# Graph network on one core: item widths chosen for two engines, and one-hots of eight small items made by one comparison

## What is computed

```python
def _graph_conv(x, src, dst, out_norm, in_norm, W, b):
    h = x * out_norm[:, None]
    agg = jax.ops.segment_sum(h[src], dst, num_segments=N_NODES)
    return agg * in_norm[:, None] @ W + b
# L0: three such layers with elu, the norms from the degrees of src and dst
# L1: msg = relu(x[src] + edge_attr @ W_edge.T + b_edge)
#     agg = segment_sum(msg, dst), then a two-layer MLP with batch norm
x = _layernorm(x + L0(x, ..., src, dst))
x = _layernorm(x + L1(x, [src, dst], edge_attr_16, ...))
```

## Time and profile before

| | |
|---|---|
| median of three runs | 6440.28 us |
| the profiled execution, own time | 6450.82 us |
| its span | 6449.1 us |
| preparation, up to the first evacuation | 123.2 us |
| counting stage | 123.2 to 2198.9 us |
| dense and gather stages | 2198.9 to 6449.1 us |
| PE busy in the span | 5397.2 us (84%) |
| DVE busy | 4675.9 us (73%) |
| POOL busy | 3568.3 us (55%) |
| ACT busy | 2313.7 us (36%) |

### The profile page before, as it was taken

One profiled execution on the slowest core, in us unless ns is written; L12 is line 12 of the kernel. 1 busy time (PEld: TensorE's weight loads), 2 busy tenths in 40 slices (PEclk: granted clock), 3 DMA queues, 4 the chain that ended last, 5 costly groups with the idle time before them and its releaser, 6 DMA issues.

```text
span 6449.1 us, 114582 instructions
## 1 busy us (share of the span) xinstructions
PE 5397.2 (84%) x38849; PEld 3248.0 (50%) x38893; DVE 4675.9 (73%) x18312; ACT 2313.7 (36%) x4022; POOL 3568.3 (55%) x3789
## 2 busy tenths in 40 slices
PE   5899997889987799999999999477787777777773
PEld 4456665556654455555555544244444444444442
DVE  4777789999999855565656622488888877777774
ACT  1776776787542100000000111243344433333331
POOL 7411112223220077777777777777777777777770
PEclk9999999999999999999999999799999988889885
DMA  2522223333211378888898987111111111111110
GB/s 81 228 96 98 83 87 114 137 119 135 86 63 52 109 264 286 279 267 278 273 274 271 281 299 260 35 44 44 43 44 43 44 41 41 41 41 41 41 39 20
DMA packets 434117, 825.45 MB, mean 128 GB/s; under 512 B 159529, under 2 KB 262981, under 8 KB 426709
## 3 DMA queue, kind: packets, MB, share of 16 engines
q1 hardware_dynamic: 305508, 713.91, 32.5%
q0 software_dynamic: 113632, 78.58, 5.5%
q10 hardware_dynamic: 14400, 25.61, 1.4%
HBM read 618.43 MB, written 199.35 MB: 127 GB/s over the span
## 4 chain that ended last, share of the span: by engine, by line
PE 37%; POOL 32%; DVE 15%; issue 11%; ACT 4%; DMA 1%; POOLq 0%; ACTq 0%; DVEq 0%
POOL rows_f L1058 26%; PE banks L2103 19%; DVE rows_f L1313 10%; PE banks L2025 7%; POOL sorted_recs L1023 5%; PE banks L1987 5%; DVE rows_f L1310 3%; ACT wide L1790 3%; PE banks L1994 2%; PE banks L2078 1%; PE banks L2085 1%; PE banks L2051 1%; PE banks L2335 1%; POOL tmp L934 1%; POOL hid L936 1%
## 5 line engine op out<-in xcount | busy, mean ns | idle before, releaser
L1058 POOL DMA_INDIRECT rows_f<-table,src_key x1725 | 1661.3, 963 | 525.5 <-issue 525.5
L1023 POOL DMA_INDIRECT sorted_recs<-onehot,rows x1280 | 1238.8, 968 | 533.4 <-issue 394.1
L1790 ACT ACTIVATE wide<-banks 128x784 fp8e4<-128x784 f32 x1563 | 1256.6, 825 | 737.3 <-PE banks L2025 733.8
L1313 DVE TENSOR_SCALAR rows_f<-rows_f,tmp 128x392 f16<-128x392 f16 (+2 forms) x5625 | 1409.5, 320 | 127.6 <-PE banks L2025 119.9
L2025 PE MATMUL banks<-rows_f 128*128 128x392 f16 (+1 forms) x6656 | 1237.6, 307 | 132.9 <-DVE rows_f L1313 124.5
L978 POOL DMA_INDIRECT onehot<-edge_runs_dram,rows_f x352 | 389.2, 1106 | 1447.5 <-DVE onehot L1166 1304.0
L2103 PE MATMUL banks<-wide,rows_f 128*128 128x512 fp8e4 (+1 forms) x4900 | 1127.4, 375 | 17.4 <-issue 12.2
L2025 PEld LDWEIGHTS banks<-rows_f 128*128 128x128 f16 x6656 | 858.6, 146 | 440.0 <-issue 163.1
L1987 PE MATMUL banks<-wide,onehot 128*128 128x392 fp8e4 x3125 | 792.6, 334 | 106.9 <-ACT wide L1790 98.7
L2192 PE MATMUL banks<-w_edge_blk,rows 80*128 80x320 f32 x690 | 293.6, 510 | 605.2 <-DVE rows_f L1610 523.9
L2103 PEld LDWEIGHTS banks<-wide,rows_f 128*128 128x128 f16 x4900 | 434.0, 98 | 396.0 <-issue 39.6
(11 more groups left out here) (334 smaller groups left out, 7046.6 us busy)
## 6 DMA issues: line engine op xcount, KB each, us to landing
wide<-counts SPq DMA_DIRECT2D x504, 896.0 KB
counts<-wide SPq DMA_DIRECT2D x50, 3136.0 KB, 9.8
rows_f<-table,src_key POOLq DMA_INDIRECT x1725
sorted_recs<-onehot,rows POOLq DMA_INDIRECT x1280
sorted_recs<-rows SPq DMA_DIRECT2D x28, 640.0 KB
rows<-attr_dram SPq DMA_DIRECT2D x345, 40.0 KB
onehot<-edge_recs_dram SPq DMA_DIRECT2D x143, 90.0 KB
agg_a<-attr_dram ACTq DMA_DIRECT2D x50, 250.0 KB
```

The costliest lines, as they stand in the source:

```text
L1023: G.indirect_dma_start(out=sorted_recs[:, :], out_offset=bass.IndirectOffsetOnAxis(ap=keys_of(t, t + 1).bitcast(I32), axis=0), in_=taken[g ...
L1058: G.indirect_dma_start(out=g_rows[:, n % ROW_RING, k, :], out_offset=None, in_=table32[:, :], in_offset=bass.IndirectOffsetOnAxis(ap=src_k ...
L1313: last = V.tensor_scalar(key, iota_key[:, 0:item.width * BLOCKS], key_cols[:, n:n + 1], None, ALU.is_equal)
L1790: A.activation(win_counts[o.half % 2][:, :, d0:d0 + o.quads * QUAD].rearrange("p b (q c) -> p b q c", c=QUAD), counted, ACT.Copy, scale=UN ...
```

## The change

Items have width 4, 2 or 1; width 8 is gone. `plan_half` takes, for each half, the least of the larger of two sums, one for each engine: items times the first number of `ITEM_COST`, and items times the second plus 4 for each node. Halves 48 to 40 keep width 4 and their items. Halves 39 to 10 have width 2 with 128 items each, 9 to 3 width 1 with 256 each, halves 2 and 1 width 2 with 256 and 337, and half 0 width 1 with 735. There are 7525 items in 59 chunks.

Items are made in **lots** of one width, 8 items (4 of width 4), in 3 buffers that hold lo and key. In a lot of width 2 or 1 one `tensor_tensor` makes all keys, with the items alternating in memory as the lo one-hots do; width 4 keeps `tensor_scalar` with contiguous columns. PE waits for a whole lot. The marks that DVE and ACT wait for are the ends of lots and octets.

Around it, more chunks ask for room: the rows are split between buffers, sets have 15 chunks, `near` is used twice, and SP loads `src_key` and `dst_key` after the search. With more items in the sparse halves, the places given by item number come at other halves: `edge_bounds` at half 30 (it was 23), `EXTREMES_TURN` 18 (21), `ROWS_TURN` 20 (27), `feature_tops` at half 26 (19), scans every 9 octets from octet 626 (every 7 from 849).

```diff
-UNITS_PER_BATCH = 6
-RING = 20
...
-ITEM_COST = {8: 14, 4: 10, 2: 9, 1: 8}
+ITEM_COST = {4: (31, 16), 2: (19, 8), 1: (14, 6)}
+NODE_COST = 4
...
-        cost = len(items) * ITEM_COST[width]
+        cost = max(len(items) * vector, len(items) * tensor + (hi - lo) * NODE_COST)
...
+LOT_CELLS, LOTS, LOT_BUFFERS = 4 * QCOLS, 8, 3
+
+SINGLE = 4
+
+
+def plan_lots():
+    lots, n = [], 0
+    while n < len(ITEMS):
+        width = ITEMS[n].width
+        size = min(LOTS, LOT_CELLS // (width * BLOCKS))
+        end = next((k for k in range(n, min(n + size, len(ITEMS))) if ITEMS[k].width != width), min(n + size, len(ITEMS)))
+        lots.append(Lot(n, end, width))
+        n = end
+    return lots
...
+MARKS = sorted({lot.end - 1 for lot in LOT_LIST} | {o.end - 1 for o in OCTETS})
...
-SETS = [(0, 1), (1, 2)] + [(c, min(c + 12, CHUNKS)) for c in range(2, CHUNKS, 12)]
+SETS = [(0, 1), (1, 2)] + [(c, min(c + 15, CHUNKS)) for c in range(2, CHUNKS, 15)]
...
+            if item.width == SINGLE:
+                key = key_ring[:, s, at * cells:(at + 1) * cells]
+            else:
+                key = lot_keys(s, cells)[:, :, at]
+            return item, lo_ring[:, s, :, at], key
+
+        def lot_keys(s, cells):
+            return key_ring[:, s, 0:cells * LOTS].rearrange("p (j n) -> p j n", n=LOTS)
...
-            rank(2 * P, SLOTS)
+            rank(2 * P, D0_SPLIT)
+            rank(D0_SPLIT, SLOTS)
...
-                if n % LOTS == 0:
-                    if lot_need(n):
-                        dve.wait_ge(s_used, lot_need(n))
-                    V.tensor_tensor(lo_ring[:, n // LOTS % LOT_BUFFERS, :, :], iota_lots,
-                                    lo_cols[:, n:n + LOTS].rearrange("p (o n) -> p o n", o=1).to_broadcast([P, P, LOTS]), ALU.is_equal)
                 item, lo, key = slot(n)
-                last = V.tensor_scalar(key, iota_key[:, 0:item.width * BLOCKS], key_cols[:, n:n + 1], None, ALU.is_equal)
-                if n in BATCH_TO:
-                    last.then_inc(s_pair, 1)
+                if n in LOT_FROM:
...
+                    if LOT_FROM[n] >= LOT_BUFFERS:
+                        dve.wait_ge(s_used, MARK_AT[LOT_LIST[LOT_FROM[n] - LOT_BUFFERS].end - 1])
+                    V.tensor_tensor(lo_ring[:, s, :, 0:size], iota_lots[:, :, 0:size],
+                                    lo_cols[:, n:lot.end].rearrange("p (o n) -> p o n", o=1).to_broadcast([P, P, size]), ALU.is_equal)
+                    if item.width != SINGLE:
+                        cells = item.width * BLOCKS
+                        V.tensor_tensor(lot_keys(s, cells)[:, :, 0:size], iota_keys[:, 0:cells, 0:size],
+                                        key_cols[:, n:lot.end].rearrange("p (o n) -> p o n", o=1).to_broadcast([P, cells, size]),
+                                        ALU.is_equal).then_inc(s_pair, 1)
+                if item.width == SINGLE:
+                    last = V.tensor_scalar(key, iota_key, single_cols[:, n:n + 1], None, ALU.is_equal)
+                    if n == lot.end - 1:
+                        last.then_inc(s_pair, 1)
...
-                    for q in range(item.at // QUAD, item.at // QUAD + units_of(item)):
...
+                    q, at = item.at // QUAD, item.at % QUAD * BLOCKS
+                    last = M(octet_ps[n % 2][:, q, at:at + item.width * BLOCKS], lo, key, start=fresh[q], stop=True, skip_group_check=True)
+                    fresh[q] = False
+                    if i in MARK_AT:
                         last.then_inc(s_used, 1)
```

More of the change, by code:

```diff
@@ L102, in plan_octets @@
     return [Octet(*o) for o in octets]
-def units_of(item):
-    return -(-item.width // QUAD)
 OCTETS = plan_octets()
[L112 to L146, removed]
+LOT_CELLS, LOTS, LOT_BUFFERS = 4 * QCOLS, 8, 3
[9 more added lines that the diff above has]
+    return lots
+LOT_LIST = plan_lots()
+LOT_FROM = {lot.begin: k for k, lot in enumerate(LOT_LIST)}
+LOT_OF = [k for k, lot in enumerate(LOT_LIST) for n in range(lot.begin, lot.end)]
+MARKS = sorted({lot.end - 1 for lot in LOT_LIST} | {o.end - 1 for o in OCTETS})
+MARK_AT = {n: k + 1 for k, n in enumerate(MARKS)}
+SINGLES = sum(item.width == SINGLE for item in ITEMS)
+SINGLE_CHUNKS = -(-SINGLES // P)
+assert all(item.width == SINGLE for item in ITEMS[:SINGLES])
+D0_SPLIT, K_SPLIT = 50 * P, 35 * P
 def plan_runs():
@@ L153, in plan_runs @@
         if item.k == 0:
-            groups.append([n, 1, item.width, item.d0])
+            groups.append([n, 1, item.width, item.d0, 0])
         else:
@@ L718, in slot @@
         def slot(n):
-            item, unit = ITEMS[n], UNIT_AT[n]
-            lo = lo_ring[:, n // LOTS % LOT_BUFFERS, :, n % LOTS]
-            key = key_ring[:, unit * QCOLS:unit * QCOLS + item.width * BLOCKS]
-            return item, lo, key
+            item, lot = ITEMS[n], LOT_OF[n]
+            s, at, cells = lot % LOT_BUFFERS, n - LOT_LIST[lot].begin, item.width * BLOCKS
+            if item.width == SINGLE:
[5 more added lines that the diff above has]
+            return key_ring[:, s, 0:cells * LOTS].rearrange("p (j n) -> p j n", n=LOTS)
         @block.sync
@@ L1786, in _ @@
                         act.wait_ge(s_insum, turn - 1)
-                act.wait_ge(s_used, BATCH_TO[o.end - 1] + 1)
+                for at in range(o.begin, o.end):
+                    if at in TURN_BEFORE:
+                        columns(TURN_BEFORE[at])
+                act.wait_ge(s_used, MARK_AT[o.end - 1])
                 d0 = o.index * OCTET
@@ L1791, in _ @@
                              ACT.Copy, scale=UNIT_COUNT, saturate=False).then_inc(s_evac, 1)
-                for at in range(o.begin, o.end):
-                    if at in TURN_BEFORE:
-                        columns(TURN_BEFORE[at])
                 if o.index == IN_AFTER and turn:
@@ L1930, in _, with columns_of @@
             pe.sem_inc(s_mlp, 1)
-            def columns_of(row, into, a, b, signal):
+            def columns_of(cells, into, a, b, signal):
                 for c in range(a, b):
-                    last = M(into[:, c:c + 1], row[0:1, c * P:(c + 1) * P], ones_f[0:1, 0:1], start=True, stop=True)
+                    last = M(into[:, c:c + 1], cells(c * P, (c + 1) * P)[0:1, :], ones_f[0:1, 0:1], start=True, stop=True)
                 last.then_inc(signal, 1)
```

133 lines of the change are left out of this document (74 added, 59 removed).

## The result

The changed kernel takes **7711.9 us** (median of four runs, 7697 to 7734), the kernel before 6440.3 beside it: a ratio of 1.1975, with an interval of 1.1938 to 1.2011. One execution of the kernel before, of 9975.6 us, is left out as a slow one. It is a fifth slower, where 6230 us was predicted. The profiled execution took 7733.5 us, its span is 7731.8.

A forecast was written before the change was run, and what follows sets the result against it. PE was taken to bound halves 39 to 26, DVE the later ones, with the round through ACT as third limit. Preparation +56 and stretches −34, −38, −84, −110 gave −210 us: 6230 us, chance 0.58, range 6180 to 6385.

The forecast's parts named there:

- Halves 39 to 26: Counting-stage stretch, width 2: four matmuls of 0.083 us on PE; 495 us with other blocks against 529, −34.
- the round: Chain of waits through ACT's evacuation, out-degree matmuls and items: 0.875 us an octet, 32.5 us a half.
- the 0.06 us of an item of width 1: PE's price for 98 columns, taken in the middle between 0.042 and 0.083 us.
- The half pace: Rival: PE reads the new keys, 16 bytes apart, at 0.79 ns a column; 6370 us, chance 0.18.
- the slower case: Rival: a stepped column costs PE more than 0.91 ns; at 1.33 ns 6822 us; chance 0.06.
- The evidence against it: L1987's two matmuls, jumping after each fourth element, take 0.51 us; four contiguous ones with as many columns take 0.50.
- The row for 0.60 us: Profile row pricing DVE's lo comparison of 1024 elements at 0.60 us from start to start.
- the −70 of the half pace: That rival's total change in us, preparation's +56 included, giving 6370 us.
- DVE's free time in a half of width 2: Argument against the coarse hand-over of lots to PE: 11 us of DVE's time are free there.
- the preparation: Ahead of the first item: POOL's rows +43 us, PE's turning and searching +13, together +56.
- the wait in `edge_bounds`: Half 30: waits for `e_max` and `e_min`, issued behind a store that takes 9.4 us to land; +9 us.
- the sum for the four stretches: Halves 39 to 26, 25 to 10, 9 to 3, 2 to 0: 495, 546, 266 and 219 to 220 us.

The follow-up runs named there:

- The table of steps: The change with keys laid out at step 8, 4, 2 or 1 in different halves of one kernel; 8620.9 us, one execution, on a chip with slow transfers.
- the version with both mended: The change with keys in pairs (step 2) and one empty item in halves 48 and 1, so every lot begins even; 6245.7 us, 0.9688 of the kernel before.

## Why the prediction was wrong

- **The step that failed** is the price on PE in *Halves 39 to 26*: "Width 2 with four matmuls of 0.083". They took 0.35 each. At full clock the four take 1.40 us, so an octet with its out-degrees takes 1.74 where the round had 0.875: PE, and not the round through ACT, sets the pace. The same price of a column, 0.42 ns for contiguous ones, stands behind the 0.06 us of an item of width 1 (0.177 measured).
- **What the rivals had.** The half pace named the 16 bytes between columns and took 0.79 ns from the weights' load; the slower case broke even at 0.91 ns and stopped at 1.33. Measured are 1.80. The mechanism had been seen and was mis-sized, and with it the chances: the load of the weights shows 0.4 ns a column more for the step, the keys 1.4 more, and I took the one for the other. The Trainium skill (SBUF — State Buffer, Door 1: The DMA port swizzle) states that two accesses in one 16-byte line are enough for the full rate. By that rule a step of 8 bytes would be free and only 16 would pay. The table of steps agrees on 16 bytes and not on 8, which already cost twice the price of 4; the measurement decides. What it shows is a price of some 1.8 ns for every 16 bytes that the read passes, however many columns it takes from them.
- **The evidence against it** was misread. L1987 reads 392 columns in fp8 as 98 groups of four, 1 byte apart within a group. It was priced by the column, as one jump in four. By the group it is 98 × 1.8 = 0.18 us, an estimate from the table of steps, and in the trace of the kernel before the first of the two takes 0.179 us to the start of the second at full clock, where 392 contiguous f16 columns take 0.165. So the row fits the price that was missing; four columns to a group hid it.
- **The clock** was in no case. At full clock an octet of width 2 takes 1.40 + 0.34 = 1.74 us, and half 29, mostly at full clock (0.94), took 61.5; half 36, at 0.50, took 72.3. The 29 halves of width 2 without `edge_bounds` took 68.5 on average ((972.0 − 89.6 + 1104.8)/29), against 34 forecast. So by this estimate some 27 us of a half's loss of 34.5 are the step and 7 or a little more the clock.
- **DVE's prices** held only for even starts. The row for 0.60 us was of lots that begin at multiples of 8; that the change shifts the lots by 53 items was not weighed. It cost nothing beside PE, but 6 us a half of width 2 with step 2 (39.9 us with odd starts, 33 to 34 with even ones).
- **Slips without weight**: the −70 of the half pace stands once for 0.79 ns a column and once for 0.84, and DVE's free time in a half of width 2 is 32.5 − 24.7 = 7.8 us by the prediction's own sum, not 11.
- **Right**: the preparation (first evacuation at 177.7, forecast 179), POOL's and PE's rows in it, the wait in `edge_bounds` (7.4 us, forecast 9), everything behind the counting stage, and, by the version with both mended, the sum for the four stretches. Halves 48 to 40 were costed at 0 and grew by 8.6 us, since the larger `find_runs` show in halves 47 and 41 (36.4 and 36.8 us, 32.0 before); the sum had 7 for that, elsewhere.

Not settled is what brings the clock down. It was low in each stretch with step 8, where PE is never idle, and full at steps 4, 2 and 1 in halves of width 2. A busy PE alone does not do it: it was busy for 526.6 of 529.0 us in the kernel before, and for 154.6 of 155.7 with step 4, both at 1.00. And half 0 of the kernel with step 1, with contiguous columns and PE busy for three quarters, had 0.56, near the lower level:

```profile
2390.80:2534.70 143.90, 106.68 (x917) 75.95 (x917) 140.54 (x208) 28.83 (x44) 16.00 (x28) 0.56 0.11 42
```

So the step is not its only cause, and no run here separates them.

## What to carry to other kernels

Before one comparison or copy is made to write several operands side by side, ask how far apart each reader then finds its neighbours: the writer's gain was 0.07 us an item here with even starts, the reader's loss 0.27. Groups of two f16 values, 4 bytes, kept nearly the full rate of both, and DVE kept its own only where the slice it reads began at an even element. A price that was read from one kind of access (a weight load, fp8, lots at multiples of 8) may be far from the price of another kind: here 0.4 ns a column stood for 1.4. With such a price in the sum, the range should reach far beyond it.

## What was new about the hardware

- A moving operand in f16 costs 0.44, 0.47, 0.92 and 1.80 ns a column with 2, 4, 8 and 16 bytes between columns, and the last did not change with the granted clock, while fp8 matmuls of 392 columns beside it went from 0.17 to 0.33 us, and 196 contiguous f16 columns from 0.086 to 0.162.
- In these numbers every 16 bytes that the moving read passes cost some 1.8 ns at either level of the clock, unless the columns in them cost more. Columns in groups of four, 1 byte apart in fp8, fit the same price a group (0.179 us for 98).
- The weight load of 128 f16 columns shows 149 ns at 16 bytes between columns and 98 at 4, the same as contiguous weights. An item of 98 columns goes from 0.062 to 0.047 us by it.
- DVE's comparison of 1568 f16 elements takes 0.885 us from start to start where the broadcast operand begins at an even element, 1.09 (step 8), 1.29 (step 4) or 1.70 (steps 2 and 1) where it begins at an odd one. With step 1 an even start does not help: 784 elements take 0.885 us instead of 0.476.
